# Moving a Newton recurrence out of the attention loop of a fused convolution, attention and expert kernel

## The chip, the cores and the metric

The kernel runs on one core of one Trainium2 chip. The metric is the time of one execution in microseconds on the device; three runs are given, and their median is the kernel's time. One more execution was recorded by the hardware profiler; its page and its trace are what the rows below come from. The engines are TensorE (PE; PEld is its weight load), VectorE (DVE), ScalarE (ACT), GpSimd (POOL) and SyncE (SP), which only issues DMAs here. Every engine works through its own instructions in the order in which the program lists them, and engines wait for each other by semaphores.

## What is computed

Six blocks one after the other, on an input of 8 images of 64 channels and 16 x 16 pixels, that is 2048 tokens of 64 channels: a non-local convolution block, a block of sign-binarised 3x3 and 1x1 convolutions, self-attention with 8 heads, a mixture of 8 experts (GELU), an attention approximated with a Haar basis, and a mixture of 16 gated experts (SiLU). Each of the last four is `t = t + block(layernorm(t))`. The part that the change is about is in the fifth block:

```
WK = jnp.linalg.pinv(W_Q)
q = x @ W_Q
k = x @ WK.T
v = x @ W_V.T
q = l2_normalize(apply_rope(q, cos, sin))
k = l2_normalize(apply_rope(k, cos, sin))
...
attn = variance_scaled_softmax(attn)
y = jnp.einsum('bts,bsc->btc', attn, v)
return y @ W_O.T
```

The pseudoinverse of the 64 x 64 matrix W_Q = A is found by Newton's recurrence `X <- f X (2 I - f A X)`, 24 times, with factors f known ahead of time. It depends on the weights alone, so it may run at any time before the fifth block's projections.

## The kernel before

The tokens stay in SBUF as a tile `T` of 128 partitions x 16 tiles x 64 channels. The program is one pass through all blocks, each written out per engine; only the attention has a loop. PSUM is `ps`, 8 banks of 128 x 512 words, given out by hand.

**Before the attention.** Products for the non-local block (L1090 to L1128), its batch norm with two tiny products (L1134, L1137), the folding of Wq and Wk (L1112, into `AH`, `AL`) and of Wv and Wu (L1141, into `GH`, `GL`), the 3x3 convolution of signs (L1149, two halves of nine products) and the 1x1 one (L1157), then transposes into `T` (L1170). ScalarE evacuates, takes signs and ReLUs, and computes the square root of the batch norm (L674).

**Layer norms.** `layer_norm(n)` on VectorE: statistics (L1477), variance, then ScalarE's Sqrt (`ln_act`, L562, with a load of its function table where the last function was of another table), reciprocal, the products `xn` (L1495) in four parts, transposes on TensorE (`ln_pe`, L780), and the split of the result into a high and a low part `XS` (L367 on ScalarE, L375 on VectorE), since matrix products here run on operands in two parts. POOL computes half of the centred values (L458).

**Attention.** `attention_steps` runs 4 rounds of 8 steps (a step is a pair of heads): a prologue, a loop of three turns of eight steps, and a tail written out. On TensorE a step holds scores (L843), keys (L819, L820), transposes of the probabilities (L854), values every fourth and fifth step (L833, L834), products with the values (L870), and the turned output (L881).

**The recurrence** is inside the loop, one iteration a step: `newton_a` (L887) makes A X in bank 6, POOL makes `nsZ` = 2f I (L502), VectorE makes Y = 2f I - f^2 A X (`nsY`, L1575), `newton_b` makes X Y and its transpose (L891, L892), and VectorE copies both (`nsX`, L1579). All are 64 x 64. After the loop one product duplicates the result over 128 partitions (L1177) and VectorE splits it (L1610, L1611) ahead of the second layer norm.

**First experts.** `gate_pe` (L793), the gate's softmax and top 2 on VectorE with an Exp on ScalarE (L572), first hidden products (L950) during it, transposes of the gates (L804), evacuation to `gT` (L578), a DMA to DRAM and broadcast loads of a row for each expert (`gates_row`, L428, L437), bias sums (L976), and then hidden (L950), GELU (L713), product with the gate row (L1622) and output (L958). Twenty products that nobody reads (`keep_clock`, L772) follow the expert block.

**Haar block.** Projections (L1033) two tiles a bank; ScalarE copies queries and keys out (L737) and their squares (L741) for each pair of tiles, VectorE copies the values (`V3`, L1218) and multiplies by the cosines from SBUF (L1204, L1205) while POOL multiplies by the sines (L480, L482); prefix sums of the values by products (L1042, L1047); coefficients; at the end far, own-block and diagonal parts are added to `T` (L1309 to L1317), the diagonal one multiplied by POOL (L485).

**Weights in two parts.** POOL splits w2 (`split_weights`, L450, L452) as soon as it is there, before the attention, and w3 (four times a cast and a subtraction) right after `ln_pool(gp, 1)`.

## Time and profile before

| | us |
|---|---|
| median of 3 runs | 439.65 |
| lowest, highest | 437.44, 440.09 |
| the profiled execution | 438.31 |
| its span, first to last instruction | 436.4 |
| TensorE busy | 361.1 (83%) |
| VectorE busy | 291.8 (67%) |
| ScalarE busy | 218.2 (50%) |
| POOL busy | 190.2 (44%) |

Busy time is the time that an engine had an instruction running, averaged over all blocks; it does not say which engine a given block waits for. For that the trace is read block by block: a row of the timeline gives the start, the duration, the engine, the line of the code and what the instruction writes and reads, and in brackets how long the engine was idle before it and what ended the wait. The clock column is the clock that TensorE was granted, 1.00 being 2.4 GHz and 0.50 being 1.2 GHz.

### The profile page before, as it was taken

Reading aid. Unit: us, or ns where it says so; the run is one execution under the profiler, and the core shown is the slowest. Engines: PE = TensorE matmul, PEld = TensorE weight load, DVE = VectorE, ACT = ScalarE, POOL = GpSimd, SP = SyncE. Lnnn points to the kernel's source line nnn. Section 1 sums busy time; section 2 is a strip of 40 time slices with the busy share of each in tenths; the row PEclk is TensorE's granted clock in tenths of the full one; section 3 lists DMA queues with packets and bytes.
Section 4 is the critical chain, followed back from the end, with each engine's and each line's share of the span. In section 5 each row is a group of like instructions: output and inputs, shape, how many; then the busy total and the mean of one; then the engine's idle time right before and its main releaser. Section 6 shows DMA issues by size and latency. Waiting matters only on the chain.

```text
span 436.4 us, 6932 instructions
## 1 busy us (share of the span) xinstructions
PE 361.1 (83%) x2145; PEld 241.9 (55%) x2147; DVE 291.8 (67%) x691; ACT 218.2 (50%) x545; POOL 190.2 (44%) x186
## 2 busy tenths in 40 slices
PE   4567269999999999998659699757258799999996
PEld 1453157777777778775446244454046356555552
DVE  2958876777777777876692566889897354444453
ACT  1524268767777776777226155450334244334432
POOL 4300025445455454545291000050100598888985
PEclk9866659999999999999956699968578999999999
DMA  7805000000000000000000992000000866445521
GB/s 236 176 0 194 0 0 1 2 2 3 0 0 0 0 0 0 0 1 2 2 0 6 361 336 74 2 0 2 1 0 11 300 217 204 178 172 187 192 96 48
DMA packets 16697, 32.79 MB, mean 75 GB/s; under 512 B 5728, under 2 KB 9504, under 8 KB 16672
## 3 DMA queue, kind: packets, MB, share of 16 engines
q1 hardware_dynamic: 16672, 32.49, 22.1%
q8 instruction: 12, 0.20, 0.2%
q14 instruction: 13, 0.11, 0.1%
HBM read 31.76 MB, written 0.72 MB: 74 GB/s over the span
## 4 chain that ended last, share of the span: by engine, by line
PE 61%; DVE 20%; ACT 8%; issue 6%; DMA 2%; POOL 1%; POOLq 1%; SPq 0%; DVEq 0%; ACTq 0%
PE ps L999 12%; PE ps L843 7%; PE ps L1007 6%; PE ps L870 6%; PE ps L854 6%; PE ps L958 4%; PE ps L950 3%; ACT va_vb L607 3%; DVE xn L1495 2%; DVE ln L1477 2%; DVE XS L375 2%; DVE negmax L1547 2%; PE ps L819 1%; PE ps L891 1%; PE ps L820 1%
## 5 line engine op out<-in xcount | busy, mean ns | idle before, releaser
L494 POOL TENSOR_TENSOR va_vb<-va_vb,rowinv 128x512 f32<-128x512 f32 x64 | 67.1, 1049 | 74.3 <-DVE rowinv L1554 74.3
L999 PE MATMUL ps<-XS,w3hl 128*128 128x512 f32 x256 | 65.7, 410 | 0.7 <-ACT gT L578 0.7
L721 ACT ACTIVATE wy<-ps 128x512 f32<-128x512 f32 x64 | 38.2, 598 | 56.1 <-PE ps L999 56.1
L607 ACT ACTIVATE va_vb<-ps,negmax 128x256 f32<-128x256 f32 x128 | 59.4, 471 | 10.6 <-DVE negmax L1547 10.2
L999 PEld LDWEIGHTS ps<-XS,w3hl 128*128 128x128 f32 x256 | 48.0, 193 | 23.0 <-DVE hid_g L1639 5.7
L1547 DVE TENSOR_REDUCE negmax<-ps 128x2 f32<-128x512 f32 x64 | 44.0, 688 | 10.2 <-PE ps L843 9.1
L843 PE MATMUL ps<-keys_gates,xcur 128*128 128x256 f32 x256 | 48.1, 311 | 2.2 <-DVE keys_gates L1539 2.2
L458 POOL TENSOR_TENSOR xn<-T,lnc 128x512 f32<-128x512 f32 x4 | 4.2, 1041 | 96.5 <-DVE lnc L1485 96.5
L843 PEld LDWEIGHTS ps<-keys_gates,xcur 128*128 128x128 f32 x256 | 35.7, 195 | 14.7 <-issue 8.1
L854 PE MATMUL ps<-consts,va_vb 128*128 128x128 f32 x256 | 40.5, 280 | 2.7 <-POOL va_vb L494 2.3
L870 PE MATMUL ps<-pT,vproj 128*64 128x256 f32 x256 | 34.5, 392 | 0.0
L854 PEld LDWEIGHTS ps<-consts,va_vb 128*128 128x128 f32 x256 | 28.5, 142 | 9.1 <-POOL va_vb L494 4.4
L598 ACT ACTIVATE keys_gates<-ps 128x512 fp32r<-128x512 f32 x32 | 19.1, 598 | 27.1 <-PE ps L820 26.8
L1639 DVE TENSOR_TENSOR hid_al<-ps,wy 128x512 f32<-128x512 f32 x16 | 11.0, 691 | 23.4 <-ACT wy L721 23.4
L607 ACT ACTIVATION_READ_ACCUMULATOR va_vb<-ps,negmax 128x1 f32 x128 | 25.7, 201 | 0.0
L1639 DVE TENSOR_TENSOR x<-ps,wy 128x512 f32<-128x512 f32 x16 | 11.1, 691 | 18.4 <-ACT wy L721 18.4
L1539 DVE TENSOR_TENSOR keys_gates<-ps,keys_gates 128x512 fp32r<-128x512 f32 x32 | 21.9, 684 | 1.5 <-ACT keys_gates L598 1.4
L591 DVE COPY pT<-ps 128x512 f32<-128x512 f32 x32 | 21.6, 675 | 1.9 <-PE ps L854 1.9
L780 PE MATMUL ps<-consts,xn 128*128 128x128 f32 x32 | 7.9, 386 | 17.1 <-DVE xn L1495 17.1
L1554 DVE RECIPROCAL rowinv<-rowsum 128x2 f32<-128x2 f32 x64 | 10.5, 164 | 15.0 <-ACT va_vb L607 14.3
L950 PE MATMUL ps<-XS,w2hl 128*128 128x512 f32 x64 | 19.9, 461 | 0.0
L870 PEld LDWEIGHTS ps<-pT,vproj 128*64 128x64 f32 x256 | 15.6, 136 | 7.6 <-issue 1.4
(305 smaller groups left out, 747.5 us busy)
## 6 DMA issues: line engine op xcount, KB each, us to landing
pT<-gates_row SPq DMA_DIRECT2D x18, 512.0 KB, 4.8
vproj<-gates_row SPq DMA_DIRECT2D x16, 512.0 KB, 4.7
gate_row_keys<-gates_row SPq DMA_DIRECT2D x14, 512.0 KB, 4.7
early<-in_f_in SPq DMA_DIRECT2D x1, 2048.0 KB, 9.1
consts<-in_consts SPq DMA_DIRECT2D x1, 816.0 KB, 5.0
x<-in_x SPq DMA_DIRECT2D x1, 512.0 KB, 3.9
w2raw<-in_f_in SPq DMA_DIRECT2D x1, 512.0 KB, 3.5
out<-in_f_out SPq DMA_DIRECT2D x1, 512.0 KB
```

The lines of the kernel that those rows point to most:

```text
L494: gp.tensor_tensor(prob[:, n % 4], prob[:, n % 4], rowinv[:, n % 4, :].unsqueeze(2).broadcast_to([P, U, N]), ALU.mult).then_inc(S("p_scale ...
L607: ins = act.activation(prob[:, n % 4, u, :], ps[:, 1 + n % 2, u * N:(u + 1) * N], ACT.Exp, bias=negmax[:, n % 4, u:u + 1], accum_out=rowsu ...
L721: act.activation(act_out[:, kk % 2, :], ps[:, 2 * (kk % 3), :], ACT.Silu).then_inc(S("f3_act"), 1)
L843: mm = pe.matmul(ps[:, 1 + n % 2, u * N:(u + 1) * N], xcur[:, g, u * P:(u + 1) * P], K[:, k % 2, n % 2, :], start=(part == 0), stop=(part ...
L854: mm = pe.transpose(ps[:, 3 + n % 2, su * N + u * P:su * N + (u + 1) * P], prob[:, n % 4, u, su * P:(su + 1) * P], ident)
L870: mm = pe.matmul(ps[h * C:(h + 1) * C, 5, 0:N], vproj[:, g, su, head * C:(head + 1) * C], pT[:, (2 * k + h) % 4, su, :], start=(k % 4 == 0 ...
L950: mm = pe.matmul(ps[:, kk % 4, :], w2hl[:, s, e], XS[:, c * CHUNK:(c + 1) * CHUNK], start=(s == 0), stop=(s == 1))
L999: mm = pe.matmul(ps[:, 2 * (kk % 3) + w, :], w3hl[:, s, e, w * HID:(w + 1) * HID], XS[:, c * CHUNK:(c + 1) * CHUNK], start=(s == 0), stop= ...
L1007: pe.matmul(ps[half, bank, :], out3[:, e, :], hid[kk % 8], start=False, stop=False, skip_group_check=True).then_inc(S("f3_out_chunk"), 1)
L1539: tt(KL[:, k % 2].rearrange("p h n -> p (h n)"), ps[:, 0, :], KH[:, k % 2].rearrange("p h n -> p (h n)").bitcast(F32), ALU.subtract).then_ ...
L1547: dve.tensor_reduce(negmax[:, n % 4, :], ps[:, 1 + n % 2, :].rearrange("p (u n) -> p u n", u=U), AX.X, ALU.max, negate=True).then_inc(S("m ...
L1639: tt(hid[kk % 8], ps[:, 2 * (kk % 3) + 1, :], act_out[:, kk % 2, :], ALU.mult).then_inc(S("f3_glu"), 1)
```

## The change

The recurrence leaves the attention loop. It becomes 48 half steps, called hops here: an even hop computes A X and adds a multiple of the identity on TensorE (two products), ScalarE copies it, scaled, as Y into `nsY`; an odd hop computes X Y and its transpose (two products), ScalarE copies both into `nsX`. The operands are now doubled over 128 partitions or columns, so weights are 128 wide, and the factor of two is taken out in the scale. VectorE and POOL no longer take part, but for six scaled identities `nsI` that POOL makes once. The start needs four loads of the transposed matrix instead of one, and the norm's product and reciprocal come early. Hops 0 to 14 stand among the work before the attention, 15 to 23 ahead of the first layer norm, 24 to 30 around the starting sums (`start_sums`) after the attention, 31 to 35 after the gate's products, 36 to 41 after the bias sums of the experts, 42 to 47 in place of the twenty products of `keep_clock`.

The split of w2 now waits for `f_prob`, that of w3 for the first gates. In the Haar block, ScalarE copies four tiles at a time and squares from SBUF, VectorE multiplies the cosines straight from PSUM, half by half, and copies the values after that; at the end the own-block weights come ahead of the diagonal ones, and the far part is added before the other two.

```diff
+        def newton_part(h):
+            return h // 2, h % 2
+        def newton_pe(pe, hops, bank):
+            for h in hops:
+                i, part = newton_part(h)
+                if part == 0:
+                    pe.wait_ge(S("nsx_ready"), i + 2)
+                    pe.matmul(ps[:, bank, 0:C], twofold(nsAT[:]), nsX[:, 2, :], start=True, stop=False)
+                    pe.matmul(ps[:, bank, 0:C], ident, nsI[:, NEWTON_SCALES.index(NEWTON_STEPS[i]), :], start=False,
+                              stop=True).then_inc(S("ns_ax"), 1)
+                else:
+                    pe.wait_ge(S("nsy_ready"), i + 1)
+                    pe.matmul(ps[:, bank, 3 * C:4 * C], twofold(nsX[:, 0:2, :]), nsY[:, 0, :], start=True, stop=True)
+                    pe.matmul(ps[:, bank, C:3 * C], twofold(nsY[:]), twofold(nsX[:, 0:2, :]), start=True,
+                              stop=True).then_inc(S("ns_xy"), 1)
+        def newton_act(act, hops, bank):
+            for h in hops:
+                i, part = newton_part(h)
+                if part == 0:
+                    act.wait_ge(S("ns_ax"), i + 1)
+                    act.activation(nsY[:], ps[:, bank, 0:C].unsqueeze(1).broadcast_to([P, 2, C]), ACT.Copy,
+                                   scale=-NEWTON_STEPS[i] ** 2 / 4).then_inc(S("nsy_ready"), 1)
+                else:
+                    act.wait_ge(S("ns_xy"), i + 1)
+                    act.activation(nsX[:].rearrange("p a c -> p (a c)"), ps[:, bank, C:4 * C],
+                                   ACT.Copy).then_inc(S("nsx_ready"), 1)
...
-            load(nsA[:], io["q3"][0:C, :], "ns_loaded")
-            load(nsAT[:], io["q3T"], "ns_loaded")
+            load(nsA[:], io["q3"], "ns_loaded")
+            for row in range(2):
+                for col_ in range(2):
+                    load(nsAT[C * row:C * row + C, col_], io["q3T"], "ns_loaded")
...
                                  ALU.mult).then_inc(S("p_scaled"), 1)
-            def newton_z(j, s):
-                gp.wait_ge(S("ns_factors"), j + 1)
-                upto(gp, "nsy_ready", j, PAIRS, s + 1)
-                gp.tensor_tensor(nsZ[:], ident[0:C, 0:C], nscoef[:, s, 1:2].broadcast_to([C, C]),
-                                 ALU.mult).then_inc(S("nsz_ready"), 1)
             def step(j, k, there):
-                if not isinstance(j, int):
-                    newton_z(j, k - 2)
...
             gp.wait_ge(S("attn_loaded"), 80)
+            gp.wait_ge(S("consts_loaded"), 16)
+            for k in range(len(NEWTON_SCALES)):
+                gp.tensor_tensor(nsI[:, k, :], con("fold"), con("newton")[:, k:k + 1].broadcast_to([P, C]),
+                                 ALU.mult).then_inc(S("nsi_ready"), 1)
+            gp.wait_ge(S("f_prob_ready"), 2)
...
             ln_pool(gp, 1)
+            gp.wait_ge(S("gates_ready"), 1)
...
-            act.wait_ge(S("folded"), 1)
-            for d in range(2):
+            act.wait_ge(S("ns_inverse"), 1)
+            act.activation(nsX[:, 2, :], nsAT[:, 0, :], ACT.Copy, scale=nsc[:, 1:2]).then_inc(S("nsx_ready"), 1)
+            act.activation(nsX[:, 0:2, :], nsA[:].unsqueeze(1).broadcast_to([P, 2, C]), ACT.Copy,
+                           scale=nsc[:, 1:2]).then_inc(S("nsx_ready"), 1)
...
+            newton_act(act, (0,), 6)
+            fold_high(0)
+            newton_act(act, (1,), 6)
+            fold_high(1)
+            newton_act(act, (2,), 6)
...
             act.activation(probT[:, 0:512], ps[:, 0, :], ACT.Copy).then_inc(S("probT_act"), 1)
+            newton_act(act, (3, 4), 6)
...
                                bias=v_("bw")).then_inc(S("wy_evac"), 1)
+                newton_act(act, ((5,), (6, 7, 8))[p], 6)
...
             act.activation(col[:, 11:14], col[:, 8:11], ACT.Sqrt).then_inc(S("bn_std_ready"), 1)
+            newton_act(act, (9, 10, 11), 6)
...
             act.activation(GH[:], ps[:, 3, :], ACT.Copy).then_inc(S("fold_high"), 1)
+            newton_act(act, (12, 13, 14), 6)
...
                            ACT.Copy).then_inc(S("T_act"), 1)
+            newton_act(act, range(15, 24), 6)
             ln_act(act, 0, ACT.Exp)
 
             attention_act(act)
+            newton_act(act, range(24, 31), 4)
             ln_act(act, 1, ACT.Exp)
+            newton_act(act, range(31, 36), 3)
...
             gate_act(act, 0, lambda: [gelu(kk) for kk in range(4)])
-            for kk in range(4, CHUNKS * EXP2):
+            for kk in range(4, 8):
+                gelu(kk)
+            newton_act(act, range(36, 42), 4)
+            for kk in range(8, CHUNKS * EXP2):
                 gelu(kk)
...
             act.activation(stream_half(0), turned_half(0), ACT.Copy).then_inc(S("T_act"), 2)
+            newton_act(act, range(42, 2 * NEWTON), 5)
             ln_act(act, 2)
...
+            for half in range(2):
+                for pair in range(2):
+                    act.wait_ge(S("qkv_ready"), 4 * half + 2 * pair + 2)
...
+                act.wait_ge(S("qk_evac"), 2 * half + 2)
+                for a in range(2):
+                    act.activation(squares[:, a, 8 * half:8 * half + 8], QK[:, a, 8 * half:8 * half + 8],
+                                   ACT.Square).then_inc(S("squared"), 1)
...
             for kk in range(4):
+                if kk == 3:
+                    pe.wait_ge(S("nsx_ready"), 18 + 2)
                 hidden(kk)
...
                 if o == 0:
                     mm.then_inc(S("b2_even_done"), 1)
+            newton_pe(pe, range(36, 42), 4)
...
             pe.wait_ge(S("attn_loaded"), 80)
+            pe.wait_ge(S("ns_inverse"), 1)
...
             pe.wait_ge(S("consts_loaded"), 16)
+            pe.wait_ge(S("nsi_ready"), len(NEWTON_SCALES))
+            newton_pe(pe, (0, 1, 2), 6)
...
                 mm.then_inc(S("f_transposed"), 1)
+                newton_pe(pe, ((3,), (4,))[p], 6)
...
                     mm.then_inc(S("wy_ready"), 1)
+                    newton_pe(pe, ((5,), (6, 7))[j // 2], 6)
             pe.wait_ge(S("bn_mean_half"), 1)
...
+            newton_pe(pe, (8,), 6)
             pe.wait_ge(S("bn_var_half"), 1)
...
+            newton_pe(pe, (9, 10), 6)
...
                                start=True, stop=True)
+                if h == HEADS // 2 - 1:
+                    newton_pe(pe, (11,), 6)
             mm.then_inc(S("folded"), 1)
+            newton_pe(pe, (12,), 6)
...
                 mm.then_inc(S("conv3_ready"), 1)
+                newton_pe(pe, ((13,), (14,))[p], 6)
...
                 mm.then_inc(S("x2_transposed"), 1)
+            newton_pe(pe, range(15, 24), 6)
             ln_pe(pe, 0)
             attention_pe(pe)
 
-            pe.wait_ge(S("nsx_ready"), NEWTON + 2)
-            pe.matmul(ps[:, 6, 0:C], eyedup[:], nsX[:, 0, :], start=True, stop=True).then_inc(S("pinv_done"), 1)
+            newton_pe(pe, range(24, 27), 4)
             pe.wait_ge(S("stream_added"), G + G * J)
-            pe.wait_ge(S("qkvw_ready"), 6)
             start_sums(pe)
+            newton_pe(pe, range(27, 31), 4)
...
             ln_pe(pe, 1)
             gate_pe(pe, 0)
+            newton_pe(pe, range(31, 36), 3)
             ffn2_pe(pe)
...
                 mm.then_inc(S("f2_turned"), 1)
 
-            keep_clock(pe, 3, 20)
+            newton_pe(pe, range(42, 2 * NEWTON), 5)
+            pe.wait_ge(S("nsx_ready"), NEWTON + 2)
+            pe.matmul(ps[:, 5, 0:C], eyedup[:], nsX[0:C, 0, :], start=True, stop=True).then_inc(S("pinv_done"), 1)
...
             def cosines(half):
-                tt(by_round(m_a, half), queries_keys(0, half), rotary("cos"), ALU.mult)
-                step(tt(by_round(m_d, half), queries_keys(1, half), rotary("cos"), ALU.mult))
+                z = projected(half)
+                cos = con("cos").rearrange("p (u g c) -> p u g c", u=U, g=G)
+                for u in range(U):
+                    for a, dst in ((0, m_a), (1, m_d)):
+                        ins = tt(by_round(dst, half).rearrange("p j (u g c) -> p j u g c", u=U, g=G)[:, :, u],
+                                 z.rearrange("p (j u) g c -> p j u g c", u=U)[:, :, u, :, a * C:(a + 1) * C],
+                                 cos[:, u].unsqueeze(1).broadcast_to([P, J // 2, G, C]), ALU.mult)
+                step(ins)
             def norms(half):
-                dve.wait_ge(S("squared"), 4 * half + 4)
+                dve.wait_ge(S("squared"), 2 * half + 2)
...
                                   ALU.add).then_inc(S("n2_ready"), 1)
-            for q in range(0, TILES, 2):
-                dve.wait_ge(S("squared"), q // 2 + 1)
-                z = ps[:, projection_bank(q), 0:384].rearrange("p (g c) -> p g c", g=2)
-                dve.tensor_copy(V3[:, q:q + 2, :], z[:, :, P:192]).then_inc(S("v3_ready"), 1)
-                if q == 8:
-                    cosines(0)
-                if q == 10:
+            for half in range(2):
+                dve.wait_ge(S("qk_evac"), 2 * half + 2)
...
             tt(p8[:], e9[:, :, :, 0:NB], blocks("below"), ALU.mult).then_inc(S("p8_ready"), 1)
+            step(tt(t9[:, :, :, 0:NB], e9[:, :, :, 0:NB], blocks("own"), ALU.mult))
+            for u in range(U):
+                ins = dve.tensor_reduce(of_u(pown[:], u), t9[:, u, :, 0:NB].rearrange("p (j g) n -> p j g n", g=G),
+                                        AX.X, ALU.add)
...
                 ins = dve.tensor_copy(of_u(pdia[:], u), e9[:, u, :, NB].rearrange("p (j g) -> p j g", g=G))
...
-            step(tt(t9[:, :, :, 0:NB], e9[:, :, :, 0:NB], blocks("own"), ALU.mult))
-            for u in range(U):
-                step(dve.tensor_reduce(of_u(pown[:], u), t9[:, u, :, 0:NB].rearrange("p (j g) n -> p j g n", g=G),
-                                       AX.X, ALU.add))
...
-            step(tt(t, t, m_a[:], ALU.add))
-            dve.wait_ge(S("diag_done"), 1)
-            step(tt(t, t, m_d[:], ALU.add))
...
             for u in range(U):
-                tt(tu[:, :, u], tu[:, :, u], ps[:, u, :].rearrange("p (j g c) -> p j g c", j=J, g=G),
-                   ALU.add).then_inc(S("haar_added"), 1)
+                ins = tt(tu[:, :, u], tu[:, :, u], ps[:, u, :].rearrange("p (j g c) -> p j g c", j=J, g=G), ALU.add)
+            step(ins)
+            step(tt(t, t, m_a[:], ALU.add))
+            dve.wait_ge(S("diag_done"), 1)
+            tt(t, t, m_d[:], ALU.add).then_inc(S("haar_added"), U)
...
             dve.wait_ge(S("T_act"), 2)
-            layer_norm(2)
+            def split_pinv():
+                dve.wait_ge(S("pinv_done"), 1)
+                raw = ps[:, 5, 0:C].rearrange("p (a c) -> p a c", a=2)
+                step(dve.tensor_copy(query_or_key(0, 1), raw))
+                tt(query_or_key(1, 1), raw, query_or_key(0, 1).bitcast(F32), ALU.subtract).then_inc(S("qkvw_ready"), 2)
+            layer_norm(2, before_low=split_pinv)
...
```

Two places in the program show how instructions moved. On TensorE, between the batch norm's last tiny product and the 3x3 convolution, before (brackets name the semaphores waited for):

```order
L1137 MATMUL ps<-col,consts 128x1 [waits bn_var_half]
L1141 MATMUL ps<-early 128x64 x8
L1149 MATMUL ps<-sgn,w3s 128x512 [waits sgn_ready,wsign_ready]
L1149 MATMUL ps<-sgn,w3s 128x512 x8
L1149 MATMUL ps<-sgn,w3s 128x512 [waits sgn_ready]
```

and in the changed kernel, where L364 and L365 are an even hop, L369 and L370 an odd one, L1188 the folding of Wv and Wu and L1199 the convolution:

```order
L1183 MATMUL ps<-col,consts 128x1 [waits bn_var_half]
L369 MATMUL ps<-nsY,nsX 128x64 [waits nsy_ready]
L370 MATMUL ps<-nsX,nsY 128x128
L364 MATMUL ps<-nsX,nsAT 128x64 [waits nsx_ready]
L365 MATMUL ps<-nsI,consts 128x64
L1188 MATMUL ps<-early 128x64 x4
L369 MATMUL ps<-nsY,nsX 128x64 [waits nsy_ready]
L370 MATMUL ps<-nsX,nsY 128x128
L1188 MATMUL ps<-early 128x64 x4
L364 MATMUL ps<-nsX,nsAT 128x64 [waits nsx_ready]
L365 MATMUL ps<-nsI,consts 128x64
L1199 MATMUL ps<-sgn,w3s 128x512 [waits sgn_ready,wsign_ready]
```

Four hops (9 to 12) now stand between the tiny product and the convolution, and the folding is cut in two around one of them.

On ScalarE, from the batch norm's table load and Sqrt to the first ReLU (`va_vb`), before:

```order
L670 ACTIVATE wy<-ps,vec 128x512 [waits wy_ready] x2
L674 ACT_TABLE_LOAD
L674 ACTIVATE col<-col 128x3 [waits bn_var_ready]
L677 ACTIVATE sgn<-x,vec 128x2x16x16 [waits x1_ready] x2
L682 ACTIVATE GH<-ps 128x512 [waits folded]
L688 ACTIVATE va_vb<-va_vb 128x512 [waits prelu_in]
```

and in the changed kernel, where L379 and L383 are the copies of even and odd hops:

```order
L383 ACTIVATE nsX<-ps 128x192 [waits ns_xy]
L379 ACTIVATE nsY<-ps 128x128 [waits ns_ax]
L722 ACT_TABLE_LOAD
L722 ACTIVATE col<-col 128x3 [waits bn_var_ready]
L383 ACTIVATE nsX<-ps 128x192 [waits ns_xy]
L379 ACTIVATE nsY<-ps 128x128 [waits ns_ax]
L383 ACTIVATE nsX<-ps 128x192 [waits ns_xy]
L726 ACTIVATE sgn<-x,vec 128x2x16x16 [waits x1_ready] x2
L731 ACTIVATE GH<-ps 128x512 [waits folded]
L379 ACTIVATE nsY<-ps 128x128 [waits ns_ax]
L383 ACTIVATE nsX<-ps 128x192 [waits ns_xy]
L379 ACTIVATE nsY<-ps 128x128 [waits ns_ax]
```

The table load now stands behind hop 8's copy, three copies stand between Sqrt and the signs, and three more (hops 12 to 14) between the evacuation of `GH` and the first ReLU, the last of which waits for products that TensorE issues after the second half of the convolution.

## Rows read from the trace of the kernel before

**Rows 1.** The page: TensorE's clock in 40 slices (tenths), and the chain by engine.
```profile
PEclk9866659999999999999956699968578999999999
...
PE 61%; DVE 20%; ACT 8%; issue 6%; DMA 2%; POOL 1%; POOLq 1%; SPq 0%; DVEq 0%; ACTq 0%
```

**Rows 2.** Stretches: busy us and instructions per engine, then clock, DMA share, GB/s.
```profile
147.70:185.00 37.30, 37.30 (x292) 28.65 (x290) 29.04 (x70) 26.91 (x87) 18.83 (x25) 1.00 0.00 0
185.00:200.46 15.46, 15.46 (x121) 12.23 (x121) 11.10 (x26) 12.95 (x43) 7.67 (x8) 1.00 0.01 2
```

**Rows 3.** Timeline, attention loop: start, us, engine, line, out<-in, count, idle before.
```profile
161.43 0.32 PE L891 MATMUL ps<-nsY,nsX 64*64 64x64 f32 x2
...
161.91 0.28 DVE L1579 COPY nsX<-ps 64x128 f32<-64x128 f32 x1 [0.20 <-PE ps L892]
```

**Rows 4.** Timeline: small products and copies at full and half clock.
```profile
15.11 2.00 PE L1112 MATMUL ps<-early 64*128 64x64 f32 x16 [0.26 <-DMA bu<-in_bu]
...
30.31 3.67 PE L1141 MATMUL ps<-early 64*128 64x64 f32 x16
...
210.32 0.66 PE L881 MATMUL ps<-consts,outT 128*128 128x64 f32 x4 [0.47 <-ACT outT L621]
...
211.08 0.29 DVE L1562 TENSOR_TENSOR T<-T,ps 128x128 f32<-128x128 f32 x1 [2.42 <-PE ps L881]
...
311.48 0.28 ACT L759 ACTIVATE p8T<-ps 128x128 f32<-128x128 f32 x1 [2.20 <-PE ps L1075]
```

**Rows 5.** Stretches of small products alone; columns as in group 2.
```profile
30.30:32.00 1.70, 1.70 (x9) 1.69 (x9) 1.17 (x6) 0.21 (x1) 0.00 (x0) 0.50 0.00 0
224.90:228.40 3.50, 3.50 (x64) 3.49 (x64) 3.27 (x15) 0.48 (x2) 3.42 (x3) 0.50 0.00 0
```

**Rows 6.** Timeline before the attention.
```profile
30.61 0.21 ACT L674 ACTIVATE col<-col 128x3 f32<-128x3 f32 x1 [2.42 <-DVE col L1399]
...
33.91 6.81 PE L1149 MATMUL ps<-sgn,w3s 128*128 128x512 bf16 x18
...
48.03 1.11 PE L1170 MATMUL ps<-consts,x 128*128 128x128 f32 x4 [1.37 <-DVE x L1435]
...
54.48 0.22 ACT L562 ACTIVATE lnc<-lnc 128x16 f32<-128x16 f32 x1 [6.87 <-DVE lnc L1487]
```

**Rows 7.** Timeline from the attention's end to the third layer norm.
```profile
210.28 1.28 ACT L562 ACT_TABLE_LOAD   x1
...
212.07 2.54 PE L936 MATMUL ps<-consts,T 128*64 128x128 f32 x32 [0.74 <-DVE qkvw L1611]
...
215.97 0.22 ACT L562 ACTIVATE lnc<-lnc 128x16 f32<-128x16 f32 x1 [4.41 <-DVE lnc L1487]
...
216.85 7.00 DVE L1495 TENSOR_TENSOR xn<-xn,lnc 128x256 f32<-128x256 f32 x4
...
228.42 3.78 PE L950 MATMUL ps<-XS,w2hl 128*128 128x512 f32 x8
...
237.80 2.23 PE L976 MATMUL ps<-gT,b2two 64*64 64x256 f32 x16
...
243.38 1.29 DVE L1622 TENSOR_TENSOR hid_al<-hid_al,pT 128x512 f32<-128x512 f32 x2 [10.63 <-DMA pT<-gates_row]
...
274.10 0.66 PE L1188 MATMUL ps<-consts,x 128*128 128x128 f32 x4 [0.23 <-DVE x L1625]
...
279.66 0.21 ACT L562 ACTIVATE lnc<-lnc 128x16 f32<-128x16 f32 x1 [3.80 <-DVE lnc L1487]
...
280.54 1.43 DVE L1495 TENSOR_TENSOR xn<-xn,lnc 128x256 f32<-128x256 f32 x4
```

**Rows 8.** Timeline, Haar stage.
```profile
288.61 1.73 DVE L1204 TENSOR_TENSOR va_vb<-theta_qk,consts 128x512 f32<-128x512 f32 x1
...
293.91 3.78 PE L1042 MATMUL ps<-f_prob,consts 128*128 128x512 f32 x4 [4.46 <-DVE f_prob L1218]
...
311.36 2.03 DVE L1302 TENSOR_TENSOR t<-e,consts 128x128 f32<-128x128 f32 x1 [0.16 <-DVE pdia L1299]
```

154 lines of the change are left out of this document (58 added, 96 removed).

## The prediction

> **What bounds the kernel now.** I read the page first. Its chain that ended last is 61% TensorE, and the clock line shows TensorE at half speed in the slices before the attention and in several later ones [rows 1]. Then I read the chain in order of time, which told me to cut the span into stages, and for each stage the timeline, to see which engine waits for which.
>
> In the attention TensorE never stops: 37.30 us busy of 37.30 in the last turn of the loop, 15.46 of 15.46 in the first half of the tail [rows 2]. There each instruction taken off TensorE is time. Outside the attention, the kernel is a chain of short steps between VectorE, ScalarE and TensorE, and TensorE's pauses are the other engines' critical work. The question is whether 48 half steps ("hops") of the recurrence fit in those pauses.
>
> **What the attention gains.** One turn of the loop has eight steps (eight pairs of heads), each with the recurrence's three products. The tail after the loop runs the same four kinds of step (plain, with value 0, value 1, turned output) without them. Loop: 37.30 / 8 = 4.66 us a step. Tail: four steps in 15.46, 3.87 us each [rows 2]. The difference, 0.80 us, is TensorE's own time for these products: a pair begins at 161.43 and its copy by VectorE at 161.91, 0.48, and the first product adds about 0.33 [rows 3]. Three turns of eight steps give 24 x (4.66 - 3.87) = 19.1; I take **-18.9**, as the first step of a turn also pays for the loop's registers. VectorE's split of the pseudoinverse leaves the end of the attention: **-0.5**.
>
> **What one hop costs.** Each is a round trip: two products on TensorE, with weights now 128 wide and 64 or 128 columns, one ScalarE copy of 128x128 or 128x192, and back. The trace of before has no such hop, but its parts:
> - Products at full clock: two products with 128-wide weights and 64 columns begin at 210.32 and VectorE starts on them at 211.08, 0.76 us.
> - At half clock: 16 passes (two a product) with 64 columns take 3.67 us against 2.00 for the same at full clock, 0.104 more a pass, 0.42 more for a hop's four. That gives 1.18; I take 1.11, since passes of a hop wait for their start more than for each other.
> - The copy: 0.28 for 128x128; 128x192 a little more, so 0.30. Back to TensorE: the products of 210.32 end at 210.98 and VectorE starts 0.10 later; for the other direction I estimate 0.07 [rows 4].
>
> Sum: 0.76 + 0.30 + 0.07 = **1.13 us at full clock, 1.11 + 0.30 + 0.07 = 1.48 at half**. Bounds: from below the 64-wide pair of [rows 3], 0.48 + 0.28 + 0.07, about 0.8; from above 1.5.
>
> **Which clock.** TensorE granted 0.50 for 1.70 us out of 1.70 busy with those 64-column products, and 0.50 for 3.50 of 3.50 busy with 8-column products [rows 5]. So small products, even back to back, did not bring the clock up, and hops are sparser still. I take half clock in all hops before the attention and after the gate's products, full clock where dense products come just before (after the attention, after the first FFN), a mixture of 1.3 in the FFN.
>
> **Site by site.** The order of ScalarE and TensorE is fixed, so a hop that is late holds whatever stands behind it on both.
>
> *Before the attention, hops 0 to 14.* Three more loads on SP's queue ahead of the constants and attention weights move the folding of Wq and Wk by about 1.3 us, and it also waits for the inverse norm. Hops 0 to 5 then stand between the transposes and products of the first stage. At half clock six hops are 8.9 us; some 2.8 fall into waits that were there, and f_prob comes 1.9 earlier, since the split of w2 no longer runs beside it: the second evacuation of wy is about 4.2 late. Hop 8, and the table load that before began during an idle stretch and now starts behind it, make Sqrt 5.3 late (30.61). Hops 9 to 12 stand before the 3x3 convolution, and ScalarE must finish 11 before the signs: 4 x 1.48 less the 2.2 that falls beside VectorE's steps, +3.7: the convolution moves from 33.91 by 9.0. Then ScalarE may not start the first ReLU until hop 14, which TensorE issues after the second half: two more waits of ScalarE and a half hop, +3.6, less 1.0 for the clock, which dense products bring up by then. So what follows the convolution is 9.0 + 2.6, about 12, late.
>
> *Hops 15 to 23* start when the transposes at 48.03 end (1.11 later, 49.14) and hold ScalarE's Sqrt, which before ran at 54.48: a pause of 5.35 [rows 6] for 9 x 1.48 = 13.3 us. +8.0. Together **+20.0** before the attention.
>
> *First layer norm after the attention, hops 24 to 30.* 211.0 (end of 210.32 + 0.66) + 3 hops 3.4 + starting sums 2.5 + 4 hops 4.5 + table load 1.3, which was over at 211.56 and now stands behind the hops, less 0.4 where the sums overlap a copy, = 222.3, where Sqrt ran at 215.97: +6.3. Against that, the split of w3 leaves this place: four xn products took 7.00 us beside it, 1.43 in the next layer norm [rows 7], -5.6. Together **+0.8**.
>
> *Hops 31 to 35* stand between the gate's products and the FFN's first ones, which began at 228.42 during VectorE's gate work. 5 x 1.48 = 7.4 (the last copy overlaps, the 0.8 above included) moves them, and with them the gates' transposes, by about **+7.4** (in place of the 0.8, not beside it).
>
> *Hops 36 to 41.* TensorE's bias sums end at 240.03 (237.80 + 2.23) and the next product waits for VectorE, which waits for gate rows until 243.38: 4.2 us of pause, for 6 x 1.3 = 7.8 less the last copy: **+3.2**. The moved split of w3, some 14 us on POOL, starts at the gates and fits in this wait and the one at 228.42.
>
> *Hops 42 to 47* follow 274.75 in place of 20 clock-keeping products; 6.8 and a table load of 1.3 end at 282.85, where Sqrt ran at 279.66: +3.2, and the split of the pseudoinverse +0.5: **+3.7** [rows 7].
>
> *Haar stage.* Cosines read PSUM, so they start before the copies are all out and no longer run beside POOL (1.73 us for 128x512, where the products of half that size at 280.54 take 0.36 each [rows 7]). But the prefix products only move from 293.91 by about 0.9, when both halves have to be evacuated. Later, own and diagonal weights change places: 2.03 us for a 128x128 product beside POOL falls to about 0.3, as at 211.08, and VectorE then waits for the far products, so 1.2 stays [rows 8]. **-2.1** (0 to -4).
>
> Sum: +20.0 - 18.9 - 0.5 + 7.4 + 3.2 + 3.7 - 2.1 = +12.8. The profiled execution took 438.31 (span 436.4); 451.1. The median of the three runs is 1.3 higher; I forecast **451**.
>
> **Rivals.**
> *A: the hops hold the clock up.* Filled pauses keep TensorE at 2.4 GHz, hops cost 1.13 and dense products in between run at full rate too. Then: before the attention +7.2 (2.3 to the sign, 9 x 1.13 - 5.35 = 4.9 after), gate +3.0, hops 36 to 41 +2.2, the rest as above: 438.3 - 5.4 = **433**, faster. For it: the clock is full in the kernel's first slices [rows 1] and lower where TensorE pauses; against: the products of [rows 5], and that one pass of 64 columns leaves most of a hop without streaming. It decides at a hop of about 1.2 us, where the total is that of before. The Trainium skill, "TensorE: Matmul & The Clock Gate", section "Why this matters for your kernels", advises against idle gaps of TensorE between bursts because they bring back the lower rate; by it this rival would hold, at 433.
> *B: hops are cheaper than their parts*, about 0.8 us as the pair in [rows 3]: then the pauses nearly hold them, and only the attention counts, **426**. Against: 128-wide weights show 0.76 for the products alone.
> *C: a mixture*, the clock high in parts (it may stay up longer at the start, and rise in the first stage or around the convolution) or stretches overlapping better than counted: **442**.
> *D: the removed clock-keeping products matter*, and hops fall to half clock also after the attention and FFN: 3 us more, **454**; part of the forecast's width.
>
> **Chances.** Forecast with D 0.65 (own range 444 to 457); C 0.18 (436 to 444); A 0.12; B 0.05. The range 434 to 457 leaves B, part of A and a tail above. About 1% is what a measurement of this kernel can tell from no change: faster 0.17, same 0.18, slower 0.65.
>
> **What would show it.** In the changed profile: attention steps at 3.87 us; hops at 1.45 to 1.5 where the clock row says 0.50 and 1.1 to 1.15 where it says 1.00; the first Sqrt of the layer norms near 74, not 54; ScalarE's idle time ended by TensorE at the hop copies; xn products of the second layer norm at 0.36 each. If the clock is 1.00 from 20 to 65 us, A is right. I am wrong if a hop at half clock costs under 1.2 us or if hops overlap with the work around them.

## The result

| kernel | median us | four runs | ratio to before, 95% interval | profiled execution: time, span, mean clock |
|---|---|---|---|---|
| before | 439.63 | 437.44 to 440.09 | | 438.31, 436.4, 0.885 |
| changed | 451.40 | 449.21 to 455.37 | 1.029 (1.020 to 1.038) | 449.21, 447.4, 0.861 |

The changed kernel is slower by 11.8 us (2.9%, well beyond the interval). The forecast was 451. The page of the changed kernel, TensorE's clock in 40 slices and the chain by engine, against [rows 1]:

```profile
PEclk9885755799999999999857599958656999999999
...
PE 49%; issue 16%; POOL 12%; DVE 10%; ACT 8%; SPq 2%; DMA 1%; POOLq 1%; DVEq 0%; ACTq 0%
```

The clock is lower ahead of the attention and in the two layer norms with hops. GpSimd, 1% of the chain before, is now 12%: without the recurrence, the chain through the attention's steps runs over GpSimd's scaling of the probabilities, though TensorE is still busy nearly all the time there, as the next section shows. The rest can be read from eight marks on ScalarE (start, duration, line): the Sqrt of the batch norm, the Sqrt of the first layer norm, the last turned output of the attention, the second Sqrt, the gates' transposes copied, the first copy of the stream behind the FFN, the third and the fourth Sqrt.

```profile
33.56 0.20 ACT L722 ACTIVATE col<-col 128x3 f32<-128x3 f32 x1
...
71.32 0.21 ACT L597 ACTIVATE lnc<-lnc 128x16 f32<-128x16 f32 x1
...
211.72 0.38 ACT L656 ACTIVATE outT<-ps 128x256 f32<-128x256 f32 x1 [3.17 <-PE ps L924]
...
223.88 0.21 ACT L597 ACTIVATE lnc<-lnc 128x16 f32<-128x16 f32 x1
...
242.27 1.10 ACT L613 ACTIVATE gT<-ps 128x512 f32<-128x512 f32 x2
...
284.38 0.60 ACT L787 ACTIVATE T<-ps 128x512 f32<-128x512 f32 x1 [0.87 <-PE ps L1236]
...
293.58 0.21 ACT L597 ACTIVATE lnc<-lnc 128x16 f32<-128x16 f32 x1
...
333.94 0.22 ACT L597 ACTIVATE lnc<-lnc 128x16 f32<-128x16 f32 x1 [8.91 <-DVE lnc L1540]
```

What ended ScalarE's idle time before a mark tells much: the first three Sqrt of the layer norms waited for VectorE in [rows 6, 7]; now no wait stands behind them, because ScalarE comes straight from a hop or a table load. The fourth, where no hop is, still waits for VectorE. The differences of neighbouring marks cut every kernel of this study into stages (us, each from its own profiled execution; BN is the batch norm, LN a layer norm; e1 to e10 are described below; the last column goes to the end of the span):

| kernel | to BN Sqrt | to 1st LN Sqrt | attention | to 2nd Sqrt | to gT | FFN | to 3rd Sqrt | Haar, to 4th | rest |
|---|---|---|---|---|---|---|---|---|---|
| before | 30.6 | 23.9 | 155.4 | 6.1 | 19.1 | 38.9 | 5.7 | 43.5 | 113.2 |
| changed | 33.6 | 37.8 | 140.4 | 12.2 | 18.4 | 42.1 | 9.2 | 40.4 | 113.5 |
| e1 loop without recurrence | 29.4 | 24.0 | 139.9 | 6.2 | 19.1 | 40.0 | 5.7 | 43.0 | 113.5 |
| e2 changed, no hops | 28.7 | 23.5 | 140.5 | 5.7 | 12.6 | 42.6 | 5.7 | 40.9 | 113.9 |
| e3 three edits | 29.1 | 23.9 | 155.4 | 6.1 | 12.6 | 42.9 | 5.7 | 40.7 | 113.4 |
| e4 dense beside hops 15 to 23 | 33.6 | 35.1 | 140.2 | 12.1 | 18.4 | 42.2 | 8.9 | 40.7 | 113.6 |
| e5 w3's split alone | 31.6 | 23.9 | 155.4 | 6.1 | 12.7 | 41.8 | 5.7 | 43.6 | 113.8 |
| e6 w3 in halves | 29.4 | 23.9 | 155.4 | 6.1 | 12.6 | 40.2 | 5.7 | 40.5 | 113.9 |
| e7 dense in pauses | 29.0 | 23.6 | 155.5 | 6.1 | 12.6 | 38.3 | 5.7 | 40.7 | 113.6 |
| e8 dense beside hops 15 to 41 | 33.4 | 36.4 | 140.2 | 13.2 | 17.4 | 40.9 | 9.7 | 41.2 | 113.5 |
| e9 Haar stage alone | 32.1 | 23.3 | 155.4 | 6.1 | 19.1 | 39.3 | 5.7 | 40.3 | 113.9 |
| e10 w2's split alone | 28.5 | 23.9 | 155.4 | 6.1 | 19.1 | 38.7 | 5.7 | 43.4 | 113.6 |

The first column scatters: four kernels whose code is the same up to the batch norm (before, e1, e5, e9) start it at 29.4 to 32.1. Where the code is the same, the other stages repeat within 0.7 us, the FFN's within 1.3; in e8 three stages of the one execution are 0.8 to 1.3 longer than in e4 without a cause in the code (in the first of them TensorE's clock came up at 46 us, during the convolution, where e4 had it from 44.4).

### The profile page after: what moved, and what is told of

Same layout as the page of the kernel before. It is cut to its first block, busy times and chain, and to the rows that moved or that the text cites. A ratio compares the mean times of both kernels' runs of the same rounds, so it can differ in the third digit from the quotient of the medians.

```text
span 447.4 us, 6886 instructions
## 1 busy us (share of the span) xinstructions
PE 379.2 (85%) x2174; PEld 265.0 (59%) x2175; DVE 267.0 (60%) x636; ACT 233.0 (52%) x591; POOL 184.4 (41%) x168
## 4 chain that ended last, share of the span: by engine, by line
PE 49%; issue 16%; POOL 12%; DVE 10%; ACT 8%; SPq 2%; DMA 1%; POOLq 1%; DVEq 0%; ACTq 0%
PE ps L1035 12%; POOL va_vb L532 11%; PE ps L1043 6%; PE ps L983 4%; PE ps L991 4%; PE ps L364 3%; PE ps L369 3%; PE ps L370 2%; SPq L416 2%; PE ps L365 2%; PE ps L847 2%; DMA bu<-in_bu 1%; PE ps L897 1%; ACT va_vb L642 1%; DVE XS L405 1%
## 5 line engine op out<-in xcount | busy, mean ns | idle before, releaser
L642 ACT ACTIVATE va_vb<-ps,negmax 128x256 f32<-128x256 f32 x128 | 59.6, 472 | 12.8 <-DVE negmax L1602 11.8
L908 PE MATMUL ps<-consts,va_vb 128*128 128x128 f32 x256 | 39.6, 278 | 4.5 <-POOL va_vb L532 4.3
L908 PEld LDWEIGHTS ps<-consts,va_vb 128*128 128x128 f32 x256 | 29.5, 142 | 10.4 <-POOL va_vb L532 8.8
L633 ACT ACTIVATE keys_gates<-ps 128x512 fp32r<-128x512 f32 x32 | 19.2, 600 | 11.0 <-PE ps L874 10.9
L383 ACT ACTIVATE nsX<-ps 128x192 f32<-128x192 f32 x24 | 7.9, 330 | 32.1 <-PE ps L370 32.1
L1671 DVE TENSOR_TENSOR x<-ps,wy 128x512 f32<-128x512 f32 x16 | 11.1, 692 | 18.4 <-ACT wy L774 18.4
L379 ACT ACTIVATE nsY<-ps 128x128 f32<-128x128 f32 x24 | 6.7, 277 | 26.9 <-PE ps L365 26.9
```

What stands on the lines that cost most here:

```text
L642: ins = act.activation(prob[:, n % 4, u, :], ps[:, 1 + n % 2, u * N:(u + 1) * N], ACT.Exp, bias=negmax[:, n % 4, u:u + 1], accum_out=rowsu ...
L908: mm = pe.transpose(ps[:, 3 + n % 2, su * N + u * P:su * N + (u + 1) * P], prob[:, n % 4, u, su * P:(su + 1) * P], ident)
L1671: tt(hid[kk % 8], ps[:, 2 * (kk % 3) + 1, :], act_out[:, kk % 2, :], ALU.mult).then_inc(S("f3_glu"), 1)
```

## The experiments

### The two halves of the change: the attention's gain and the hops' price

e1_loop_off, on the kernel before (in the step of TensorE and of VectorE; GpSimd's `newton_z` and the wait for the finished inverse go too; the kernel leaves out the recurrence):

```diff
-                in_loop = not isinstance(j, int)
+                in_loop = False
```

> The kernel before with the recurrence of the pseudoinverse left out of the attention's loop (so the inverse stays at its first guess); all else as before. It shows what the attention alone gains. Theory 1 (the step is bound by TensorE and the round trips of the softmax, as the trace of the changed kernel suggests): a loop step takes 4.04 us instead of 4.67, 24 steps save 15.1, so about 424.5 us. Theory 2 (the forecast's term): the steps run at 3.87 us as in the first half of the tail, 18.9 saved, 420.7 us; then something else in the changed kernel slows its attention.

Measured: 424.50 us (422.71 to 425.18), ratio 0.966 (0.963 to 0.968). That is 15.1 less, as the first theory says. In a full turn of the loop, the stretch from one product with the values to the one eight steps later (columns as in [rows 2]), the changed kernel's and this one's:

```profile
154.14:186.48 32.34, 31.72 (x241) 24.63 (x240) 24.48 (x52) 27.17 (x88) 16.86 (x16) 1.00 0.00 0
186.48:202.29 15.81, 15.58 (x122) 12.33 (x121) 11.71 (x27) 13.40 (x45) 8.33 (x8) 1.00 0.01 2
```

```profile
136.50:168.80 32.30, 31.70 (x246) 24.64 (x242) 24.59 (x53) 27.07 (x86) 16.93 (x17) 1.00 0.00 0
```

A step takes 32.34 / 8 = 4.04 us in the changed kernel and the same in e1, so nothing else in the change disturbs the attention. TensorE has 31.72 us of work in it; before it had 37.30 in a turn [rows 2]. Its share of the recurrence was 5.6 a turn, 0.70 a step, not 0.80, and the other 0.62 us of a turn are new waits, nearly all of them for GpSimd's scaling, by the groups of lines of the changed kernel in this turn (count, busy, mean ns, idle before and its releaser):

```profile
L908 PE MATMUL ps<-consts,va_vb 128*128 128x128 f32 x65 | 10.1, 275 | 0.6 <-POOL va_vb L532 0.5
```

e2_no_hops, on the changed kernel, in both `newton_pe` and `newton_act` (the two waits for a later hop wait for the first guess; the kernel leaves out the recurrence):

```diff
-            for h in hops:
+            for h in ():
```

> The changed kernel with all 48 hops left out (the inverse stays at its first guess); its loads, scales, splits and Haar stage as changed. The distance to the changed kernel is what the hops cost. Theory 1 (hops lie on the path): the attention gives 15.1, the moved split of w3 about 5.6, the Haar stage 2 to 3, the split of w2 1 to 2, the added loads take back about 1: 439.6 - 24 = about 416 us, so that the hops cost 35 us, 0.74 us each. Theory 2 (hops are mostly hidden and something else, such as the moved splits or the Haar order, eats the gain): above 430 us.

Measured: 416.70 us (415.83 to 417.00), ratio 0.948 (0.946 to 0.950), as the first theory says. So the 48 hops cost 451.4 - 416.7 = 34.7 us, 0.72 each and 1.45 an iteration, where the loop did an iteration for 15.1 / 24 = 0.63. From its row of the table, by stage: hops 0 to 8 4.9, hops 9 to 23 14.3, hops 24 to 30 6.5, hops 31 to 35 5.8, hops 36 to 41 nothing (-0.5), hops 42 to 47 3.5.

### What dense products beside the hops do to the clock

Two kinds of hop, from the changed kernel's timeline of ScalarE, hops 16 and 17 and hops 43 and 44 (start, us, in brackets the idle time before and what ended it):

```profile
60.14 0.28 ACT L379 ACTIVATE nsY<-ps 128x128 f32<-128x128 f32 x1 [1.20 <-PE ps L365]
61.73 0.33 ACT L383 ACTIVATE nsX<-ps 128x192 f32<-128x192 f32 x1 [1.31 <-PE ps L370]
...
286.67 0.33 ACT L383 ACTIVATE nsX<-ps 128x192 f32<-128x192 f32 x1 [0.80 <-PE ps L370]
287.75 0.28 ACT L379 ACTIVATE nsY<-ps 128x128 f32<-128x128 f32 x1 [0.75 <-PE ps L365]
```

At the first place the granted clock is 0.50, a hop takes 1.53 and 1.59 in turn, 1.56 on average; at the second it is 1.00 and a hop takes 1.08. e4_fill2, on the changed kernel, behind each of hops 15 to 23:

```diff
+                for _ in range(2):
+                    pe.matmul(ps[:, 3, :], w3s[:, 0, :], sgn2[:, 0:512], start=True, stop=True)
```

> The changed kernel with two dense products of 128x512 (bf16, into a bank that nobody reads) behind each of hops 15 to 23, all at half clock in the changed kernel, 1.56 us a hop. Theory 1 (the sparse products of the hops are what leaves the clock low, dense ones bring it up): after two or three hops the granted clock is 1.00, a hop takes 1.1 to 1.3 us, the Sqrt of the layer norm before the attention comes at 69 to 72 us (71.3 now), total 447 to 452 us. Theory 2 (the clock stays low here whatever TensorE does): each hop takes about 2.0 us, 4 us more in all, 455 us.

Measured: 446.84 us (446.14 to 448.03), ratio 1.017 (1.014 to 1.019), and the Sqrt at 68.72. Its stretches around hops 15 to 18, and hops 19 and 20 with the fillers on TensorE between them:

```profile
57.00:60.00 3.00, 2.95 (x13) 2.42 (x13) 2.72 (x16) 0.33 (x1) 0.00 (x0) 0.50 0.00 0
60.00:62.00 2.00, 2.00 (x10) 1.49 (x11) 1.86 (x16) 0.28 (x1) 0.03 (x1) 0.63 0.00 0
62.00:64.00 2.00, 2.00 (x13) 1.15 (x12) 1.63 (x2) 0.61 (x2) 1.01 (x1) 1.00 0.00 0
```

```profile
64.18 0.33 ACT L385 ACTIVATE nsX<-ps 128x192 f32<-128x192 f32 x1 [0.80 <-PE ps L370]
...
65.06 0.59 PE L373 MATMUL ps<-sgn,w3s 128*128 128x512 bf16 x2
...
65.26 0.28 ACT L381 ACTIVATE nsY<-ps 128x128 f32<-128x128 f32 x1 [0.75 <-PE ps L365]
```

The clock goes from 0.50 to 1.00 within this stretch, and the hop falls to 1.08 although 0.59 us of dense products now stand in each: they lie wholly in the round trip. The first theory holds; the time and the Sqrt even came a little below its ranges (447 and 69). In the changed kernel the same hops kept TensorE busy for 2.85 of 4.00 us, at 0.50 throughout:

```profile
60.00:64.00 4.00, 2.85 (x11) 2.26 (x11) 3.04 (x13) 0.89 (x3) 1.04 (x1) 0.50 0.00 0
```

The stage gets 2.7 us shorter in the profiled executions (37.8 to 35.1); that the medians differ by 4.6 is probably in part the scatter of the changed kernel's own runs (449.2 to 455.4). The kernel stays slower than before: at full clock too each of these hops is a round trip of 1.08 us on the path.

e8_fill_more adds the same behind hops 31 to 41:

```diff
-            newton_pe(pe, range(31, 36), 3)
+            newton_pe(pe, range(31, 36), 3, fill=2, spare=2)
-            newton_pe(pe, range(36, 42), 4)
+            newton_pe(pe, range(36, 42), 4, fill=2, spare=5)
```

> The kernel of e4_fill2 (dense products behind hops 15 to 23), and the same two dense products behind each of hops 31 to 41 too. Theory 1 (the clock of these hops is the same matter): hops 31 to 35 fall from 1.56 to between 1.1 and 1.3 and the FFN's first products run at full rate, 2 to 3 us less than 446.8; hops 36 to 41 give nothing, as they end before the gate rows come: 444 us. Theory 2 (there the pause is set by something else): 446 to 448 us.

Measured: 445.89 us (444.90 to 447.75), ratio 1.014 (1.009 to 1.019). From hop 34 on they take 1.08 (the copies of hops 33, 34 and 35):

```profile
234.35 0.33 ACT L385 ACTIVATE nsX<-ps 128x192 f32<-128x192 f32 x1 [1.21 <-PE ps L370]
235.43 0.28 ACT L381 ACTIVATE nsY<-ps 128x128 f32<-128x128 f32 x1 [0.75 <-PE ps L365]
236.51 0.33 ACT L385 ACTIVATE nsX<-ps 128x192 f32<-128x192 f32 x1 [0.80 <-PE ps L370]
```

The gates' stage and the FFN's are 1.0 and 1.3 shorter than in e4, other stages of this execution are longer, and the medians differ by 0.9, between the two theories. Of the FFN's 1.3, 0.9 is not the clock: VectorE's first two gating products start 0.9 into a GpSimd instruction here, and take 2.56 where they take 3.48 in e4 (the next section explains this collision). So this says only that the gain is small: three of the five hops have passed before the clock is up.

### The three other edits, alone and together

e3_moves is the kernel before with the two splits of weights at their new times and the Haar stage of the change; the recurrence stays in the loop.

```diff
+            gp.wait_ge(S("f_prob_ready"), 2)
             split_weights(gp, w2hl, ...)
...
+            gp.wait_ge(S("gates_ready"), 1)
             split_weights(gp, w3hl, ...)
```

> The kernel before, with the recurrence left in the attention's loop, and only three other edits of the change: both weight splits at their new times and the Haar stage from PSUM. Theory 1 (these edits are worth the same without the hops): -5.6 in the layer norm after the attention, -2 to -3 in the Haar stage, about -1.5 before the attention: 429 to 431 us. Theory 2 (the split of w3 fitted only because hops make the pauses longer, now it delays gates or hidden rows of the FFN by its 14 us on GpSimd): 434 to 438 us, with VectorE's gating products or gate rows late.

Measured: 431.20 us (430.44 to 432.51), ratio 0.981 (0.978 to 0.983): faster than both kernels. The time is the first theory's, but the collision that the second one names is there too. The gates come 6.5 us earlier (12.6 for 19.1), the Haar stage takes 2.8 less, but the FFN takes 4.0 more. Its first gating products on VectorE, and GpSimd in the same time:

```profile
235.39 3.99 DVE L1637 TENSOR_TENSOR hid_al<-hid_al,pT 128x512 f32<-128x512 f32 x2 [10.66 <-DMA pT<-gates_row]
...
236.17 2.66 POOL L452 TENSOR_TENSOR w3hl<-early,w3hl 128x1024 fp32r<-128x1024 f32 x1
```

Two products take 3.99 instead of 1.29 [rows 7]: 2.70 more, the length of GpSimd's last subtraction, 2.66. The split of w3 ends at 238.8, and the gate rows are there at 235.4. The changed kernel has the same collision:

```profile
251.13 3.46 DVE L1649 TENSOR_TENSOR hid_al<-hid_al,pT 128x512 f32<-128x512 f32 x2 [11.21 <-DMA pT<-gates_row]
...
251.38 2.67 POOL L484 TENSOR_TENSOR w3hl<-early,w3hl 128x1024 fp32r<-128x1024 f32 x1
```

In the five kernels in which this subtraction starts within 0.8 us of the pair (changed, e2, e3, e4, e5), the pair ends 0.54 or 0.55 us behind the subtraction: 239.38 and 238.83 in e3, 254.59 and 254.05 in the changed kernel. In e8 the first product starts 0.92 into it, takes 1.96 and ends at 252.64, again 0.54 behind its end at 252.10. The product waits for the end of GpSimd's instruction, wherever in its course it came.

The Trainium skill, "SBUF — State Buffer", section "Who interferes with whom", says that the pair of ports shared by VectorE and GpSimd is an exclusive lock, and that a VectorE instruction with two inputs in SBUF contends with a GpSimd instruction that reads SBUF. Both are the case here, and a product that waits until the GpSimd instruction is over agrees with it.

e6_halves, on e3_moves:

```diff
+            split_weights(gp, w3hl, w3raw, [slice(e, e + 4) for e in (0, 4)], ...)
             ln_pool(gp, 1)
             gp.wait_ge(S("gates_ready"), 1)
-            split_weights(gp, w3hl, w3raw, [slice(e, e + 4) for e in range(0, EXP3, 4)], ...)
+            split_weights(gp, w3hl, w3raw, [slice(e, e + 4) for e in (8, 12)], ...)
```

> The kernel of e3_moves with the split of w3 in two halves: two of its four parts right behind the attention's last scaling, ahead of the layer norm's work on GpSimd (which waits there for 8 us), two at the gates, so that they end some 3 us before the first gate rows come. Theory 1: the first gating products start beside nothing, take 0.65 us each, and about 4 us come back: 427 us (431.2 for e3_moves). Theory 2 (the late products of the FFN have another cause, the gate rows themselves): 431 us, unchanged; or slower if the parts behind the attention slow VectorE's statistics.

Measured: 428.47 us (427.96 to 429.44), ratio 0.975 (0.970 to 0.979), the fastest kernel of the study that computes the whole result, with e7 below. The last subtraction is over at 231.9, and the first products are as fast as before:

```profile
229.59 2.35 POOL L452 TENSOR_TENSOR w3hl<-early,w3hl 128x1024 fp32r<-128x1024 f32 x1
...
236.16 1.29 DVE L1638 TENSOR_TENSOR hid_al<-hid_al,pT 128x512 f32<-128x512 f32 x2 [11.20 <-DMA pT<-gates_row]
```

So the collision was the cause of the late products, as the first theory says, but 2.7 of the 4.0 us come back (FFN 40.2), not all. The other 1.3 are not explained; runs of the same FFN differ by as much (38.9 before, 40.0 in e1).

e5_w3_only, on the kernel before:

```diff
+            gp.wait_ge(S("gates_ready"), 1)
             split_weights(gp, w3hl, ...)
```

> The kernel before with one edit: the split of w3 waits for the gates of the first FFN, as in the changed kernel. Theory 1 (from the trace of the run with three edits: the layer norm after the attention is rid of GpSimd, but the split's last part then runs beside the first gating products of VectorE): 6.5 us less up to the gates, 4.0 more before the FFN's products run on, net -2.5, 437 us; the first two gating products take 4 us instead of 1.3. Theory 2 (the forecast's: the split fits in the waits there): -5.6, 434 us.

Measured: 435.69 us (434.75 to 436.51), ratio 0.991 (0.988 to 0.994): 4.2 less, between the two theories, in the profile -6.4 up to the gates and +2.9 in the FFN.

e9_haar_only is the kernel before with the change's Haar stage alone (the cosines' part of the edit; the rest is that of the change):

```diff
-                tt(by_round(m_a, half), queries_keys(0, half), rotary("cos"), ALU.mult)
+                        ins = tt(by_round(dst, half).rearrange(...)[:, :, u],
+                                 z.rearrange(...)[:, :, u, :, a * C:(a + 1) * C], ...)
```

> The kernel before with one edit: the Haar stage of the changed kernel (products of the rotation straight from PSUM, own and diagonal weights in other order). Theory 1 (what the traces of all kernels with this edit show between the Sqrt of the third and of the fourth layer norm, 40.4 to 40.9 us against 43.5): -2.8 to -3.1, 436.9 us. Theory 2 (the forecast's term): -2.1, 437.7 us. Theory 3 (part of it comes only when the split of the pseudoinverse and the split of w3 have moved too): above 438.5 us.

Measured: 437.10 us (434.42 to 440.58), ratio 0.996 (0.993 to 0.998), 2.0 to 2.2 less; its stage is 3.2 shorter in the profiled execution (40.3). The medians cannot tell 2.1 from 3.

e10_w2_only, on the kernel before:

```diff
+            gp.wait_ge(S("f_prob_ready"), 2)
             split_weights(gp, w2hl, ...)
```

> The kernel before with one edit: the split of w2 waits until VectorE has made the second half of f_prob. Theory 1 (the sum of the single edits closes: 8.4 for all three, less 4.2 for w3 and 2.9 for the Haar stage): -1.3, 438.5 us, with f_prob 1.5 to 2 us earlier and part of that on the path. Theory 2 (f_prob was not on the path): no change, 439.8 us.

Measured: 437.41 us (436.24 to 440.42), ratio 0.996 (0.993 to 0.998), 1.8 to 1.9 less, a little more than the first theory's 1.3. The two products that make `f_prob` are rid of the same collision: they took 3.44 us beside the split of w2 in the kernel before, and 2.86 to 3.44 in three of the four kernels with the early split (1.29 in e1, where they came first), and take 1.29 here.

```profile
18.53 1.29 DVE L1381 TENSOR_TENSOR f_prob<-f_both,f_col 128x512 f32<-128x512 f32 x2
```

Over all profiled executions without hops, the Sqrt of the batch norm starts at 28.9 on average where w2's split is late (five kernels) and at 30.9 where it is early (four). The three edits alone add up to 4.0 + 2.0 + 1.8 = 7.8 by the ratios and 4.2 + 2.2 + 1.9 = 8.3 by the medians, together they gave 8.4, and with the attention's 15.1 they give 416.1 against 416.7 in e2_no_hops: the account closes within 1 us.

### Dense products in pauses without hops

e7_warm, on e6_halves:

```diff
+            keep_clock(pe, 3, 12)
             ln_pe(pe, 0)
...
+            keep_clock(pe, 4, 20)
             pe.wait_ge(S("out_loaded"), 64)
...
+            keep_clock(pe, 5, 9)
             pe.wait_ge(S("haar_added"), U)
```

> The kernel of e6_halves with dense products of 128x512 (bf16, into banks that nobody reads) in three pauses of TensorE: 12 before the transposes of the layer norm ahead of the attention, 20 behind the bias sums of the first FFN, 9 before the starting sums behind the Haar stage. Theory 1 (dense products in a pause bring the clock up for what comes behind it): the first steps of the attention 2 to 3 us shorter, the FFN's first output products 1 to 1.5, the starting sums 2 (4.70 at half clock): 420 to 422 us. Theory 2 (the clock falls again before the work comes, or the fillers themselves are late): 426 to 429 us.

Measured: 428.62 us (426.85 to 429.13), ratio 0.976 (0.971 to 0.980): no gain over e6. Its stretches ahead of the attention:

```profile
50.00:52.00 2.00, 0.91 (x5) 0.20 (x2) 1.86 (x12) 0.00 (x0) 0.57 (x1) 1.00 0.00 0
54.00:56.00 2.00, 1.34 (x8) 0.69 (x8) 1.92 (x6) 1.58 (x6) 1.08 (x1) 1.00 0.00 0
56.00:58.00 2.00, 1.22 (x4) 0.93 (x4) 1.91 (x5) 1.83 (x5) 1.48 (x2) 0.54 0.00 0
60.00:62.00 2.00, 2.00 (x10) 2.00 (x11) 0.69 (x1) 0.11 (x1) 0.00 (x0) 0.50 0.00 0
```

The clock came up, and it had fallen again before the attention's dense part began; the stage took 155.5 as ever. So far the second theory holds. The third place went by the first: with the nine dense products right ahead of them, the starting sums behind the Haar stage ran at 1.00 and took 2.57 us, instead of 4.49 in e6, most of it at 0.50:

```profile
307.24 2.57 PE L947 MATMUL ps<-consts,T 128*64 128x128 f32 x32 [0.89 <-DVE T L1337]
```

```profile
309.53 4.49 PE L947 MATMUL ps<-consts,T 128*64 128x128 f32 x32 [3.96 <-DVE T L1334]
```

But the next Sqrt waits for VectorE's statistics, not for the sums, and the stage takes 40.7 as against 40.5 in e6: faster products off the path gave nothing. In the FFN, at the second place, the clock stayed up (1.00 from 228 to 244, where e6 has 0.50 from 232 to 240) and the profiled stage is 1.9 shorter; the medians don't show it, so whether this is worth anything stays open.

## Why the prediction was right, and where it was not

The direction and the mechanism came out as said: the hops lie on the path and cost more than the attention gains. So did the size, but partly by luck, because two errors cancelled. Per term, in us, against the stages above (the first row compares averages, 33.5 over the three kernels with hops, 30.9 and 28.9 over those without, since this stage scatters):

| term | forecast | measured |
|---|---|---|
| up to the batch norm's Sqrt (w2's split included) | +5.3 | +2.6 (hops +4.6, w2 -2.0) |
| from there to the first layer norm's Sqrt | +14.7 | +13.9 |
| attention | -18.9 | -15.1 |
| hops 24 to 30 | +6.3 | +6.5 |
| split of w3 away from the layer norm | -5.6 | -6.5 there, +4.0 in the FFN |
| attention's end to the gates in all (the two rows above, hops 31 to 35 and the -0.5) | +6.9 | +5.3 (25.2 before, 30.6 now) |
| hops 36 to 41 | +3.2 | 0; the FFN's 3.2 are the split of w3 |
| hops 42 to 47 with the pseudoinverse's split | +3.7 | +3.5 |
| Haar stage | -2.1 | -2.0 by medians, -3.1 by stage |

**What one hop costs: right at full clock, a little low at half.** 1.13 was said for full clock, 1.08 measured; 1.48 for half, 1.56 measured. The sum of products, copy and two hand-overs held.

**Which clock: the step that failed ahead of the batch norm.** The forecast took half clock for all hops before the attention. The changed kernel's stretches there:

```profile
24.00:26.00 2.00, 2.00 (x12) 2.00 (x11) 0.57 (x1) 0.65 (x2) 0.00 (x0) 0.50 0.00 0
26.00:28.00 2.00, 2.00 (x12) 1.79 (x12) 1.32 (x3) 0.97 (x3) 0.00 (x0) 0.89 0.03 8
...
32.00:34.00 2.00, 0.94 (x6) 0.74 (x6) 0.48 (x3) 1.95 (x4) 0.00 (x0) 0.81 0.00 0
34.00:36.00 2.00, 1.97 (x9) 1.85 (x9) 1.85 (x6) 0.28 (x1) 0.00 (x0) 0.50 0.00 0
```

Transposes and products stand between hops 2 to 5 and fill TensorE (4.00 of 4.00 us busy from 24 to 28), the clock comes up at 26.4, and hops 5 to 8 run at full clock; it falls at 33.3, while hop 9's copy stands behind the table load and TensorE does 0.94 us of work in two. So mixture C was true for this stretch; around the convolution's second half, where hops 13 and 14 had 1.00 too, the forecast had counted it. From 57 to 72 and from 222 to 240 the clock was 0.50 throughout, and the first Sqrt of the layer norms came at 71.3, not near 74.

The rows behind the forecast's choice were also thinner than it took them for: in the kernel before, the 1.70 us of small products at 0.50 [rows 5] are followed by the dense ones of the convolution, which were at 0.50 as well:

```profile
34.00:38.00 4.00, 4.00 (x10) 1.38 (x11) 3.08 (x14) 1.20 (x2) 0.00 (x0) 0.50 0.66 223
```

So they say little of whether it is small products that leave the clock low; the changed kernel from 57 to 72 and e4 show it.

**The attention: the term was mis-sized.** The forecast took 3.87 us a step from the first half of the tail in [rows 2]. The kernel before again, that half cut at the starts of the products with the values, one step and three:

```profile
184.99:188.50 3.51, 3.51 (x30) 2.81 (x29) 2.45 (x6) 2.26 (x8) 1.44 (x2) 1.00 0.00 0
188.50:200.46 11.96, 11.96 (x93) 9.42 (x93) 8.66 (x21) 10.69 (x36) 6.24 (x6) 1.00 0.01 2
```

The first step took 3.51, the others 3.99 each. I read it as slack, which no run isolates: while TensorE was the bound, the other engines had their parts ready, and one step could live on that. In steady state a step is 4.04, as e1 and the changed kernel show, and 24 x (4.67 - 4.04) = 15.1 is the measured gain. The forecast put its 0.80 us down to the recurrence's products alone; a step has 0.70 us less TensorE work, and 0.08 of new waits take a part of that back.

**The split of w3: "fits in this wait" was wrong.** Its 14 us start with the gates at 240.0 and end at 254.0, 2.9 us behind the arrival of the gate rows. The forecast's +3.2 for the FFN was right as a number and wrong as a cause: e2, without hops, has the same 42.6. Hops 36 to 41 end at 254.7, beside this collision, and cost nothing here. With the split out of the way they would have cost some 2.5 (an estimate: TensorE ends their last product at 254.3, and the first gating product, which is all that TensorE's next product needs, is done at 251.8); no run has the hops and w3's split in halves.

**Loads on SP's queue.** Folding starts 2.0 later (15.11 in [rows 4]), where 1.3 was said, but one pair of executions cannot tell these apart: over the eight kernels without the three added loads it starts at 14.9 to 17.9, 16.0 on average, over the four with them at 16.7 to 17.1, 16.9 on average.

```profile
17.12 2.00 PE L1153 MATMUL ps<-early 64*128 64x64 f32 x16 [1.62 <-DMA bu<-in_bu]
```

**xn and the Haar stage** went as said: the four products of the second layer norm take 1.43 instead of 7.00, the cosines read PSUM in 0.41 each, and the product for the own weights 0.28 instead of 2.03 [rows 7, 8]:

```profile
224.48 1.43 DVE L1548 TENSOR_TENSOR xn<-xn,lnc 128x256 f32<-128x256 f32 x4
...
304.73 0.41 DVE L1259 TENSOR_TENSOR va_vb<-ps,consts 128x256 f32<-128x256 f32 x1
...
322.81 0.28 DVE L1353 TENSOR_TENSOR t<-e,consts 128x128 f32<-128x128 f32 x1
```

**The rivals.** A (hops hold the clock up, 433) fell: they do not from 57 to 72. Where dense products made hops run at full rate, in e4 and e8, the kernel stood at 446.8 and 445.9. What e8 has left at half clock is hops 0 to 4, 9 to 12, 15 to 17, 31 to 33 and 45 to 47, some seventeen; by 0.48 that is 8 us, and the convolution's first half (4.05 us in e8; the second half took 2.19 at full clock in the changed kernel) would give up to 2 more. So with all hops at full clock the kernel would take some 436 to 438 (an estimate from these rows, not run): near the time before, and above A's 433. The Trainium skill, "TensorE: Matmul & The Clock Gate", section "Why this matters for your kernels", advises against idle gaps of TensorE. That is not enough here: from 57 to 72 TensorE never waited longer than 0.42 us between the hops' products, and the clock stayed at 0.50; dense products in the same gaps brought it up, in e4. And the clock of nine hops was worth 3 to 5 us where the hops in all cost 35. B fell by the 1.08. C held for one stretch, as said. D (the removed clock-keeping products) is seen in little: hop 30 and the last two of hops 42 to 47 ran at half clock (1.53 to 1.58), three times 0.48 and not 3 us, and in e2, where those products are gone too, the stage up to the third Sqrt is 5.7 as before.

In gross terms the forecast had the hops at 41.2 (20.0 + 1.9 + 6.3 + 6.6 + 3.2 + 3.2) where they cost 34.7, the attention at 18.9 where it gave 15.1, and the other edits at 9.6 (1.9, 5.6 and 2.1) where they gave 8.4: 6.5 too much on one side, 5.0 on the other.

## What to carry to other kernels

A chain of small dependent products costs its round trips wherever nothing hides it: 0.63 us an iteration within a stage whose TensorE is busy anyway, 1.45 in pauses that other engines' chains had made, since engines with a fixed order then wait for the chain too. Before moving work into a pause, ask which engine the pause belongs to, and whether the moved chain is shorter than what that engine is waiting for. When a bound engine is relieved, take the new step time from steady state, several steps behind the change of regime, and look for the waits that then appear; and when GpSimd's work on SBUF moves, look at what VectorE starts from SBUF within its last instruction.

## What the runs showed of the hardware

- The same chain of small products ran at both levels: at 1.00 for 7 us (26.4 to 33.3) behind a stretch in which other products filled TensorE, and for four hops behind the FFN; at 0.50 from 57 to 72 us with TensorE busy for 10.9 of 15. With 0.59 us of dense products in each round trip it was granted full rate there too, and lost no time to them (1.08 us a hop with them in e4, and without them behind the FFN).
- A full clock reached in a pause did not outlast it: at 1.00 from 50 to 56 us, 0.54 from 56 to 58, with TensorE busy 1.22 of 2.00 (e7). Where the dense products ended right ahead of the work, it lasted: the starting sums took 2.57 us at 1.00 and 4.49 at 0.50 (e7, e6). Dense products that go on up to the attention were not tried.
- A VectorE product of 128x512 with both operands in SBUF, 0.65 us alone, waited out a GpSimd subtraction of 2.66 us (3.99 for two in e3), and in six kernels a product so held up ended 0.54 or 0.55 us behind the subtraction.
- The first 30 us, with some 200 GB/s of loads, scatter by 2.7 us between executions of the same code (29.4 to 32.1 for the batch norm's Sqrt); a difference of 1 us there needs several profiles.
